# Row sends of a mixture-of-experts router: a wait, inside a phase, for the landing of the first-choice send of the tile ahead

## The chip, the core and the metric

One core of one Trainium2 chip runs one program. The metric is the device time of one execution in microseconds (us). The engines are PE (TensorE), DVE (VectorE), ACT (ScalarE), POOL (GpSimd) and SP (SyncE, which here only issues DMAs). They run side by side and meet only through semaphores. 16 DMA engines move data; SP's DMAs go out on one queue, those of POOL on another, whose descriptors POOL makes itself (the profile calls it software_dynamic).

## The reference, cut to what matters

```python
x = x + 0.5 * L0_moe(layernorm(x))            # 8 experts, 2 choices per token
x = x + L0_attention(layernorm(x))            # keys and values at half length
x = x + 0.5 * L0_moe(layernorm(x))
x = x + 0.5 * L1_ffn(x)     # causal attention, then experts, with residuals inside
x = x + L1_attention(x)                       # causal
x = x + 0.5 * L1_ffn(x)

# the experts of L1_ffn: 16 experts of capacity 2*T/16 = 512 rows
top1, top2 = argmax(logits), argmax(logits without top1)
loc1, loc2 = rank of the token among those of its expert, first and second choices
xin  = rows of xt, token t in row slot(t, choice) of its expert (dropped beyond capacity)
eout = gelu(xin @ fc1 + b1) @ fc2 + b2        # per expert
out  = g1 * eout[slot1] + g2 * eout[slot2]
```

There are 8 x 512 = 4096 tokens of 128 floats, so 32 tiles of 128 tokens.

## The kernel before, in words

The program is a row of blocks: a first routing, experts, attention with half-length keys, experts, causal attention (32 units), experts, two causal attentions as one pipeline (64 units), experts, and the last sums. The change touches the two causal attention blocks alone, at their ends, and both by the same code.

**A unit** is one batch entry (512 tokens) and one of four groups of four heads. `order(u)` writes by hand what each engine does in unit u. PE computes 12 score tiles of unit u (L784, with masks L651) and, unless u is one of the last two, 12 tiles for the row maxima of unit u + 2 (L668). ACT turns each score tile into exponentials (L863), DVE reduces each maxima tile (L1013), and PE multiplies the exponentials with the values (L728). Score and maxima tiles each go through a ring of three PSUM banks, so PE can be at most three tiles ahead of ACT and of DVE. For the next unit, ACT copies the maxima out (nm, L895), POOL splits them into three bf16 parts (`max_split`, L1160 to L1166), and SP writes these into the query rows (L1290); PE waits for that before the first score tile of a unit.

**The routing** of the experts that follow is laid into the same pipeline. Tokens are taken in phases, `SENT_PHASES` = tiles 0 to 7, 8 to 15, 16 to 19, 20 to 23, 24 to 27 and 28 to 31. For each phase DVE chooses experts (`choose`), PE counts ranks (`ranks`), and DVE makes the row numbers (`find_ranks`, slot, L403 and L405). Then `send` lets POOL scatter the rows of each tile from SBUF to `xe_rows` in DRAM, by two indirect DMAs (L418): the one for the first choice raises `first_sent` by 16 when it has landed, the one for the second choice raises `second_sent[j]`. A send is 128 rows of 512 bytes. POOL takes its instructions in order, so what stands behind a send waits for it. Before the first tile of a phase POOL waits for the row numbers and, from the second phase on, for the landing of all second-choice sends of the phase ahead.

**Where the sends stand** is the table `SENT_IN`: tiles 0 to 7 one to a unit, in units -13 to -6 counted from the end; then tiles 8 to 10 in unit -5, 11 to 13 in -4, 14 and 15 in -3, 16 to 19 in -2 and 20 to 23 in -1, behind the unit's other POOL work. Tiles 24 to 27 and 28 to 31 go out behind the last unit, when the row numbers are there. The experts' block begins on SP with `fetch_sent`, which waits for all sends.

Of the kernel before, what the change touches and what calls it, by code (L numbers as in the profile page):

```python
# [408 lines left out]
def send(pool, k, r, j, tiles):  # L409

    s, (a, b) = k.sig, r.phases[j]
    for t in tiles:
        if t == a:
            pool.wait_ge(*s.slots_ready.at(j + 1))
            if j:
                pool.wait_ge(*s.second_sent[j - 1].at(16 * (a - r.phases[j - 1][0])))
        for c, signal in ((0, s.first_sent), (1, s.second_sent[j])):
            pool.indirect_dma_start(k.xe_rows[:, :], bass.IndirectOffsetOnAxis(k.slot[:, c, t:t + 1], 0),  # L418
                                    k.xn[:, t * P:(t + 1) * P], None, bounds_check=r.slots - 1,
                                    oob_is_err=False).then_inc(signal.h, 16)  # L420
# [93 lines left out]
def attention(nc, k, segments, r):  # L514
# [122 lines left out]
    with nc.Block() as block:  # L637
# [486 lines left out]
        def _(pool):  # L1124
# [90 lines left out]
            for u in range(U):  # L1215
# [29 lines left out]
                if r.sent and u - U in SENT_IN:  # L1245
                    phase, first, end = SENT_IN[u - U]
                    send(pool, k, r, phase, range(first, end))
            if r.sent:
                for j in (LAST - 1, LAST):
                    send(pool, k, r, j, range(*r.phases[j]))  # L1250
# [788 lines left out]
```

## Time and profile before

| | us |
|---|---|
| median of 3 runs | 1927.85 (1926.94 to 1928.74) |
| the profiled execution | 1924.9 |
| its span, first to last instruction | 1923.2 |
| PE / DVE / ACT / POOL busy | 1566.6 / 1307.4 / 968.5 / 1075.7 |
| indirect sends on POOL (L418) | 128 instructions, 127.6 us busy |
| mean granted TensorE clock | 0.881 of full |

The span is that of the profiled execution; 1.7 us of its time lie around it. No engine is busy all the time, so a share of busy time says little here; each stage has to be read for itself. A unit's time can be read as the step from one `nm` (L895) to the next. In a wait's row the name behind the arrow is what released the wait; "issue" means that nothing the profile shows was missing, and "remote" that no instruction of this core was found that ended just then.

### The profile page before, as it was taken

The page shows a single profiled execution, that of the slowest core. Times are in us where ns is not written, and L with a number is a line of the kernel's source. Part 1 is how long each engine was busy: PE and PEld are TensorE (multiplying, and loading weights), DVE is VectorE, ACT ScalarE, POOL GpSimd, SP SyncE. Part 2 cuts the span into 40 slices and gives each one's busy share as a digit, 9 for nine tenths or more (in the row PEclk, how much of TensorE's full clock was granted, in tenths as well). Part 3 has the DMA queues.
Part 4 walks back from the last instruction along what each step waited for, and adds up shares of the span by engine and source line. Part 5 has one row for each costly group of instructions (what it writes and reads, how often), then busy time and mean ns, then how long its engine had stood idle before and what let it go on. Part 6 is the DMA issues. An engine that isn't in the chain of part 4 may idle for free. (4 is left out here: it accounts for less than half of the span.)

```text
span 1923.2 us, 46440 instructions
## 1 busy us (share of the span) xinstructions
PE 1566.6 (81%) x17682; PEld 948.8 (49%) x17682; DVE 1307.4 (68%) x3414; ACT 968.5 (50%) x2039; POOL 1075.7 (56%) x1712
## 2 busy tenths in 40 slices
PE   5548888875599998875899599999999998776992
PEld 4532333344345555544576255555555555435772
DVE  7348887883678887856321688888888887765224
ACT  4124667642156676642233177677777766431331
POOL 3446667414477857664355377455666766651552
PEclk9976899987689999985799599999999999865996
DMA  8342323203433322210343433232332323101545
GB/s 295 109 133 86 103 69 94 79 26 94 133 101 113 94 82 83 80 37 19 115 136 102 137 119 91 81 112 82 100 97 82 95 90 97 37 22 55 150 124 159
DMA packets 233187, 188.24 MB, mean 98 GB/s; under 512 B 30035, under 2 KB 221306, under 8 KB 232326
## 3 DMA queue, kind: packets, MB, share of 16 engines
q1 hardware_dynamic: 222582, 166.36, 29.0%
q0 software_dynamic: 10240, 18.89, 3.1%
q8 instruction: 142, 2.33, 0.5%
q14 instruction: 79, 0.65, 0.1%
q10 hardware_dynamic: 144, 0.00, 0.0%
HBM read 104.34 MB, written 80.74 MB: 96 GB/s over the span
## 5 line engine op out<-in xcount | busy, mean ns | idle before, releaser
L1013 DVE TENSOR_REDUCE mx<-PS 128x2 f32<-128x512 f32 (+3 forms) x1408 | 784.6, 612 | 207.1 <-PE PS L651 138.9
L863 ACT ACTIVATE pt<-PS 128x512 f32<-128x512 f32 (+2 forms) x1408 | 668.7, 537 | 323.7 <-PE PS L651 220.2
L668 PE MATMUL PS<-ka,qa 52*128 52x256 bf16 (+3 forms) x2048 | 469.3, 309 | 69.5 <-DVE mx L1013 51.5
L784 PE MATMUL PS<-qa,ka 55*128 55x512 bf16 (+3 forms) x1792 | 465.6, 324 | 31.0 <-DMA qa<-nm 21.2
L728 PE MATMUL PS<-pt,vs 128*32 128x512 f32 (+3 forms) x3584 | 359.4, 487 | 11.7 <-ACT pt L863 7.0
L651 PE MATMUL PS<-mask_q,identh 64*128 64x64 bf16 x3072 | 300.5, 193 | 2.1 <-issue 2.1
L651 PE MATMUL PS<-mask_k,identh 64*128 64x64 bf16 x3072 | 299.5, 192 | 1.6 <-issue 1.6
L784 PEld LDWEIGHTS PS<-qa,ka 55*128 55x128 bf16 x1792 | 167.8, 95 | 261.3 <-ACT pt L863 103.3
L651 PEld LDWEIGHTS PS<-mask_k,identh 64*128 64x128 bf16 x3072 | 249.9, 97 | 53.2 <-issue 10.2
L651 PEld LDWEIGHTS PS<-mask_q,identh 64*128 64x128 bf16 x3072 | 253.4, 98 | 32.5 <-issue 10.6
L668 PEld LDWEIGHTS PS<-ka,qa 52*128 52x128 bf16 x2048 | 172.7, 95 | 101.2 <-DVE mx L1013 65.6
L1160 POOL CAST nm<-nm 16x128 bf16<-16x128 f32 x128 | 35.9, 280 | 324.7 <-ACT nm L895 312.4
L418 POOL DMA_INDIRECT xe_rows<-xn,slot x128 | 127.6, 997 | 84.0 <-DVE slot L405 41.6
L1422 ACT ACTIVATE pt<-PS,f1b 128x512 f32<-128x512 f32 x128 | 87.7, 687 | 154.6 <-PE PS L1386 150.8
L1398 PE MATMUL PS<-pt 128*128 128x128 f32 x1280 | 155.3, 279 | 9.1 <-ACT pt L1422 6.8
L1386 PE MATMUL PS<-pt 128*128 128x512 f32 (+1 forms) x384 | 157.2, 556 | 4.6 <-DVE pt L1479 1.8
L1398 PEld LDWEIGHTS PS<-pt 128*128 128x128 f32 x1280 | 150.7, 196 | 11.7 <-issue 11.1
L1524 POOL DMA_INDIRECT y_rows<-pt,idx x80 | 79.3, 991 | 116.6 <-DVE pt L1489 98.4
L728 PEld LDWEIGHTS PS<-pt,vs 128*32 128x32 f32 x3584 | 83.5, 111 | 92.5 <-issue 40.8
L1386 PEld LDWEIGHTS PS<-pt 128*128 128x128 f32 x384 | 75.0, 206 | 59.7 <-issue 51.5
L1479 DVE TENSOR_SCALAR pt<-PS,l2w,l2b 128x512 f32<-128x512 f32 x32 | 25.9, 810 | 101.1 <-PE PS L1376 98.0
L1516 POOL DMA_INDIRECT pt<-xn_rows,idx x32 | 31.2, 974 | 97.4 <-issue 56.2
(249 smaller groups left out, 2357.0 us busy)
## 6 DMA issues: line engine op xcount, KB each, us to landing
pt<-in_f_w SPq DMA_DIRECT2D x96, 256.0 KB
qa<-q_parts SPq DMA_DIRECT2D x256, 96.0 KB
ka<-k_parts SPq DMA_DIRECT2D x192, 96.0 KB
q_parts<-parts SPq DMA_DIRECT2D x32, 384.0 KB
k_parts<-parts SPq DMA_DIRECT2D x24, 384.0 KB, 2.6
xn<-y_rows SPq DMA_DIRECT2D x32, 256.0 KB, 3.1
hid<-y_rows SPq DMA_DIRECT2D x32, 256.0 KB, 3.6
q_parts<-parts SPq DMA_DIRECT2D x32, 256.0 KB
```

The lines of the kernel that those rows point to most:

```text
L418: pool.indirect_dma_start(k.xe_rows[:, :], bass.IndirectOffsetOnAxis(k.slot[:, c, t:t + 1], 0), k.xn[:, t * P:(t + 1) * P], None, bounds_c ...
L651: mm = pe.matmul(PS[:, bank, col + j * HALF:col + (j + 1) * HALF], k.identh[half * HALF:(half + 1) * HALF, j, :], table[half * HALF:(half ...
L668: mm = pe.matmul(PS[:, bank, i * n:(i + 1) * n], k.qa[rows, b % 2, g, h // 2, qb * P:(qb + 1) * P], k.ka[rows, b % 2, g, h // 2, 0:n], sta ...
L728: mm = pe.matmul(PS[32 * h:32 * h + 32, O_BANK, q0:S], k.vs[:, g, kb, h, :], k.pt[:, u % 2, at[c] + i * n:at[c] + (i + 1) * n], start=(kb ...
L784: mm = pe.matmul(PS[:, bank, i * n:(i + 1) * n], k.ka[rows, b % 2, g, h // 2, kb * P:(kb + 1) * P], k.qa[rows, b % 2, g, h // 2, q0:S], st ...
L863: nc.scalar.activation(k.pt[:, u % 2, at[c]:at[c] + len(heads) * n], PS[:, SC_BANK + c % RING, 0:len(heads) * n], ACT.Exp, scale=SCORE_SCA ...
L1013: nc.vector.tensor_reduce(out, PS[:, MX_BANK + t % RING, 0:len(heads) * n] .rearrange("p (h n) -> p h n", n=n), AX.X, ALU.max).then_inc(s. ...
L1160: pool.tensor_copy(hi, full).then_inc(s.nm_hi.h, 1)
L1386: pe.matmul(PS[:, H_BANK + f, 0:capacity], k.w1[:, par, f * P:(f + 1) * P], k.xeT[:, par, 0:capacity], start=True, stop=True).then_inc(s.h ...
L1398: mm = pe.matmul(PS[:, Y_BANK + par, t * P:(t + 1) * P], k.hT[:, par, f, t * P:(t + 1) * P], k.w2[:, par, f, :], start=(f == 0 and t == 0) ...
L1422: nc.scalar.activation(k.hT[:, e % 2, f, 0:capacity], PS[:, H_BANK + f, 0:capacity], GELU, bias=w.b1[:, e * FC + f:e * FC + f + 1]).then_i ...
L1524: pool.indirect_dma_start(k.y_rows[:, :], bass.IndirectOffsetOnAxis(k.idx[:, 1, n:n + 1], 0), k.ys[e % RING_E][:, t, :], None).then_inc(s. ...
```

## The change

Inside a phase, each tile but the phase's first one gets a wait on POOL ahead of its two sends, in all phases but the last (tiles 28 to 31). `first_sent` must have reached 16 times the tile's number, that is, all first-choice sends of the tiles ahead must have landed.

```diff
             pool.wait_ge(*s.slots_ready.at(j + 1))
             if j:
                 pool.wait_ge(*s.second_sent[j - 1].at(16 * (a - r.phases[j - 1][0])))
+        elif j < len(r.phases) - 1:
+            pool.wait_ge(*s.first_sent.at(16 * t))
         for c, signal in ((0, s.first_sent), (1, s.second_sent[j])):
             pool.indirect_dma_start(k.xe_rows[:, :], bass.IndirectOffsetOnAxis(k.slot[:, c, t:t + 1], 0),
                                     k.xn[:, t * P:(t + 1) * P], None, bounds_check=r.slots - 1,
```

Each of the two blocks gets 23 such waits: 7 for phase 0, 7 for phase 1, and 3 for each of phases 2, 3 and 4. No instruction that computes or moves data is added, removed or put elsewhere.

## Rows read from the trace of the kernel before

**Rows 1.** The page, costliest groups: the sends (busy, mean ns, idle before, releaser).

```profile
L418 POOL DMA_INDIRECT xe_rows<-xn,slot x128 | 127.6, 997 | 84.0 <-DVE slot L405 41.6
```

**Rows 2.** Windows: stretch, length, busy us of PE, PEld, DVE, ACT, POOL, clock, DMA.

```profile
745.00:815.00 70.00, 60.27 (x906) 35.11 (x907) 54.55 (x129) 42.68 (x95) 45.89 (x82) 0.93 0.29 89
815.00:885.00 70.00, 53.01 (x578) 29.38 (x579) 38.99 (x145) 29.72 (x66) 40.23 (x52) 0.76 0.10 33
...
1555.00:1640.00 85.00, 75.11 (x1131) 43.56 (x1131) 66.00 (x151) 53.64 (x119) 58.00 (x101) 0.94 0.29 88
1645.00:1722.00 77.00, 59.34 (x639) 31.84 (x632) 46.89 (x168) 33.22 (x73) 43.85 (x59) 0.78 0.09 28
```

**Rows 3.** Waits, 815 to 885 us: who, for whom, us in total, times, longest.

```profile
ACT pt L863 <- remote: 18.4, 6, 7.3
...
DVE mx L1013 <- remote: 9.8, 3, 4.4
...
ACT xfT L215 <- remote: 6.9, 1, 6.9
...
DVE rw L390 <- remote: 5.6, 1, 5.6
...
ACT nm L895 <- remote: 3.1, 1, 3.1
```

**Rows 4.** Waits, 1645 to 1722 us, the same columns.

```profile
ACT pt L863 <- remote: 22.0, 6, 5.9
...
DVE mx L1013 <- remote: 10.3, 3, 6.2
...
ACT xfT L215 <- remote: 5.8, 1, 5.8
```

**Rows 5.** Waits, 745 to 815 us: the only row with "remote".

```profile
DVE mx L1013 <- remote: 0.5, 1, 0.5
```

**Rows 6.** Waits, 1555 to 1640 us: the only such row of ACT.

```profile
ACT pt L863 <- remote: 1.6, 1, 1.6
```

**Rows 7.** Timeline of POOL: first-choice sends of tiles 4 and 5 (start, us, idle before).

```profile
779.52 1.00 POOL L418 DMA_INDIRECT xe_rows<-xn,slot  x1 [0.78 <-POOL parts L1140]
...
783.89 1.01 POOL L418 DMA_INDIRECT xe_rows<-xn,slot  x1 [0.16 <-issue]
```

**Rows 8.** Timeline of POOL: first-choice sends of tiles 8 and 9, the next max_split.

```profile
817.20 1.00 POOL L418 DMA_INDIRECT xe_rows<-xn,slot  x1 [1.62 <-issue]
...
819.78 0.97 POOL L418 DMA_INDIRECT xe_rows<-xn,slot  x1 [0.30 <-issue]
...
828.80 0.28 POOL L1160 CAST nm<-nm 16x128 bf16<-16x128 f32 x1 [4.21 <-ACT nm L895]
```

**Rows 9.** Timeline of ACT in the same burst.

```profile
823.08 0.38 ACT L863 ACTIVATE pt<-PS 128x256 f32<-128x256 f32 x1 [3.67 <-remote]
```

**Rows 10.** The DMA view, 839 to 843 us: bytes moved, in 40 slices of 0.1 us.

```profile
GB/s 0 0 0 0 271 292 41 0 0 0 0 0 0 0 0 0 0 410 246 0 0 0 0 0 0 0 0 0 0 0 466 98 0 0 0 0 0 0 0 0
```

**Rows 11.** Timeline of POOL: last send of tile 13, the max_splits behind and next.

```profile
840.45 0.97 POOL L418 DMA_INDIRECT xe_rows<-xn,slot  x1 [0.30 <-issue]
841.41 0.28 POOL L1160 CAST nm<-nm 16x128 bf16<-16x128 f32 x1
...
855.32 0.28 POOL L1160 CAST nm<-nm 16x128 bf16<-16x128 f32 x1 [7.17 <-ACT nm L895]
```

**Rows 12.** Timeline of POOL: last send of tile 23, first of tile 24.

```profile
1718.90 0.97 POOL L418 DMA_INDIRECT xe_rows<-xn,slot  x1 [0.30 <-issue]
1721.85 1.06 POOL L418 DMA_INDIRECT xe_rows<-xn,slot  x1 [1.98 <-DMA xe_rows<-xn,slot]
```

**Rows 13.** Timeline of POOL: first send of the last phase.

```profile
910.53 1.14 POOL L418 DMA_INDIRECT xe_rows<-xn,slot  x1 [15.56 <-DVE slot L405]
```

**Rows 14.** The score matmuls (L784), 815 to 885 us: all that ended PE's idle time.

```profile
  ACT pt L863: 11.8, 9
  issue: 4.6, 11
```

## The prediction

> **What bounds the kernel now.** I read the page first. No engine is busy all through, so the question is only what happens where the 128 sends stand [rows 1]. The sends lie in two places, one at the end of each causal attention. So the second view is the table of windows over these ends. Each end has a stretch with isolated sends (one tile, two sends, per unit) and one with bursts (two to four tiles in a row). From the one to the other ACT's busy time falls from 42.7 to 29.7 us of 70 in the first block, and from 53.6 of 85 to 33.2 of 77 in the second; DVE and PE fall too, and the DMA engines are busy for 10% [rows 2]. So in the bursts no compute engine is the bound, and neither is DMA bandwidth. Part of that is sound: the last two units have no maxima tiles, and the routing of the last phases stands there. The third view, the waits, shows the rest. With the bursts ACT waits 18.4 + 6.9 + 3.1 = 28.4 us in the first block for something that the profile can't name [rows 3], and 22.0 + 5.8 = 27.8 us in the second [rows 4]. With isolated sends, 8 tiles in each block, the whole is 0 us for ACT in the first [rows 5], where only DVE has such a row, and 1.6 us in the second [rows 6]. DVE shows the same: 15.4 and 10.3 us in the bursts, 0.5 us outside in the first block [rows 3 to 5].
>
> The fourth view, the timelines, shows how one such stall looks. In the burst of tiles 8 to 10 ACT sits idle for 3.67 us and runs at 823.08 [rows 9]. By the pitch of the tiles (819.78 - 817.20 = 2.58 us [rows 8], two sends each, so 1.29 us from send to send) the last two sends of this burst start at about 822.4 and 823.6. So while POOL sends one tile after another, work that is ready on other engines isn't taken up, for several microseconds, and it goes on near the time at which some send lands. I can't tell from the trace what carries the stall. What I can read is its price: the bursts of tiles 8 to 23 cost ACT 28.4 / 16 = 1.8 and 27.8 / 16 = 1.7 us per tile, isolated tiles at most 1.6 / 8 = 0.2.
>
> The Trainium skill speaks against this. "SBUF — State Buffer", section "SBUF: two separate sides", says that engine ports and DMA ports are apart, so that a transfer can't slow a compute instruction; the exception it names is the port pair that VectorE and GpSimd share. The trace shows ACT stalled as well as DVE, which that exception doesn't cover. By the page the stalls would have another cause than the transfers in flight, and spacing the sends would give nothing: that is the rival "no change" below.
>
> **The change part by part.** It adds 23 waits per block and removes nothing.
>
> *Waits that are met anyway.* Tiles 1 to 7 are sent one to a unit; the closest two start 783.89 - 779.52 = 4.37 us apart [rows 7]. Tiles 11 and 14 open a unit. These 9 waits per block find their landing done and cost nothing, as long as a landing takes under 4.37 us.
>
> *Waits inside a burst.* These are tiles 9, 10, 12, 13, 15, 17, 18, 19, 21, 22 and 23, so 11 per block, and 3 more (25 to 27) behind the last unit. Now the pitch is the 2.58 us of rows 8. When does a send land? Its bytes move 1.55 us after its start: the send of 840.45 fills the slices at 842.0 and 842.1, and the two before it show the same spacing [rows 10, 11]. And there is one place where POOL already waits for nothing but a landing: tile 24's first send starts 1721.85 - 1718.90 = 2.95 us after the start of the send on whose landing it waited [rows 12]. That is the price of a wait of this kind, waking and issuing included. So the pitch of a tile goes from 2.58 to 2.95 us, by 0.37 us, if the wait for the first-choice send wakes POOL at once. The other end: the second-choice send of the tile ahead starts some 1.3 us after the first and is still in flight then. If POOL, like ACT in the stalls, is only released when that one has landed as well, the pitch is 1.3 + 2.95 = 4.25 us, by 1.7 us more than now. The cost of the wait is so between 0.37 and 1.7 us; it can't be below nothing, since it only holds POOL back. I take 0.37, because the released engines of rows 9 ran on in mid-burst, with further sends in flight.
>
> *What is queued behind.* POOL's next work behind a burst is max_split. Behind tiles 8 to 10 it waits 4.21 us for ACT anyway [rows 8], which covers 2 x 0.37 (and, just, 2 x 1.7). Behind tiles 14 and 15 it waits 7.17 us [rows 11]. Behind tiles 11 to 13 it starts with no idle time, at 841.41, so it comes 0.7 to 3.4 us later; who waits for it is SP and then PE's first score tile of the unit after, and that is far: the next max_split is at 855.32, and PE's scores never waited for these rows in the whole stretch [rows 11, 14]. Without that cover it would cost 0.7 us per block. Behind tiles 16 to 23 POOL has only more sends. Tiles 24 to 27 would end 3 x 0.37 later plus what tiles 21 to 23 pass on, 2.2 us in all, at most 10; the last phase waits 15.56 us for DVE's row numbers anyway [rows 13]. The last phase itself has no new wait, so what the experts' block waits for isn't held back. So on POOL, SP and the last phase the change costs nothing.
>
> *What the spacing gives.* The only thing to win is the stall. Between two prices per tile (1.75 us at a pitch of 2.58, at most 0.2 us, say 0.1, at 4.37 and more) I go on a straight line: at 2.95 us a tile costs 1.75 - 1.65 x 0.37 / 1.79 = 1.41 us, so each wait gives 0.34 us, and 22 of them 7.5 us. There is a reason for more than the line: the rings of three tiles let ACT and DVE catch up after a short stop and not after a long one, and the bytes of two tiles now come 1.29 us apart throughout a burst, and 1.29 + 0.37 = 1.66 us apart at every wait with the change. I add a third and take 10 us. At the other end, pitch 4.25, the line gives 22 x 1.54 = 34 us.
>
> The sum against the profiled execution: 1924.9 - 10 + 0 = 1914.9 us. The median of the runs shown lies 2.95 us above that execution, so against the median it is 1927.85 - 10 = 1917.8 us.
>
> **The rivals.**
>
> *A, the forecast:* the pitch grows little, the stalls shrink a little. 4 to 16 us off, 1917.8.
>
> *B, isolated tiles:* POOL is released late, as ACT is, and the sends go out as in rows 7. 34 us off: 1894. For it speaks that ACT's and DVE's stalls of 3 to 7 us [rows 3, 4] must come from signals that are held up, and POOL's wait is such a signal too. Against it, that a landing is itself what seems to end a stall.
>
> *C, no change:* the landing is early. Bytes move 1.55 us after the start and the next tile starts at 2.58, so if POOL takes the wait up ahead of time, it never sees it, and the pitch stays; or the pitch grows and the same number of sends stalls the others for as long in total, since each is as long in flight as before. Then 1927.85. The skill's "DMA: Bandwidth & Descriptors", section "Anatomy of one DMA — SWDGE (gpsimd) path", gives about 2.0 us fixed plus bytes / 436e3 us per DMA; for 64 KB that would be an estimated 2.15 us, also under 2.58. Rows 12 have 2.95 for landing, waking and issuing.
>
> *D, slower:* the stalled share stays and the bursts grow. The bursts of tiles 8 to 23 last some 40 us per block (16 tiles at 2.58, less the idle time between), and ACT stalls for 28.4 of them, 0.7. If that share holds for the added time as well, 22 x 0.37 x 0.7 = 5.7 us are lost: 1933.5. At a pitch of 4.25 it would be 22 x 1.7 x 0.7 = 26 us, 1954. It decides from the point where ACT's unnamed waits in the two burst stretches go over the present 28.4 + 27.8 us: then the stall belongs to POOL's making of sends for its length, and not to their closeness.
>
> **How the numbers follow.** A measurement of this kernel can tell about 0.2%, 3.9 us, from no change. Chances: A 0.37, B 0.2, C 0.26, D 0.17. The bottom of A lies at the limit, so I give faster 0.55, same 0.28, slower 0.17. The point is A's, 1917.8. The range leaves out D but for its lower edge and takes in all of B, with 4 us for the line: 1890 to 1933.5. The likeliest case alone is 1912 to 1924.
>
> **What would show it right or wrong.** In the timeline of POOL, the pitch of tiles 8 to 10: 2.95 (A), 4.25 (B), 2.58 (C). In the waits of the two burst stretches, ACT's "remote" sum: about 46 to 50 us in both blocks for A, under 15 for B, 56 for C, over 60 for D. The units with bursts should be shorter, and the idle time before 910.53's send should still be over 5 us. It would be wrong if POOL's wait were held up in one burst and not in another, or if the freed time in the last units were given back in the wait for the last phase's row numbers, which DVE makes behind everything else.

## The result and the profile after

| | us |
|---|---|
| before, median of 5 runs | 1928.74 (1926.94 to 1937.12) |
| after, median of 5 runs | 1911.12 (1908.49 to 1915.54) |
| ratio, 95% interval | 0.9898, 0.9873 to 0.9922 |
| the profiled execution after, its span | 1912.18, 1910.5 |
| PE / DVE / ACT / POOL busy after | 1556.0 / 1307.4 / 968.9 / 1077.0 |
| mean granted TensorE clock after | 0.887 of full |

The change makes the kernel 1.0% faster, 17.6 us between the medians and 12.7 us between the two profiled spans. In the first block the bursts stand at nearly the same times as before; in the second they start 2 us and end 8 us earlier. The same windows hold them in both kernels. Of the page of the kernel after, the row of the sends, to be read against [rows 1] (busy, mean ns, idle before, main releaser):

```profile
L420 POOL DMA_INDIRECT xe_rows<-xn,slot x128 | 129.0, 1008 | 78.6 <-issue 42.3
```

The idle time before the sends did not grow, it is 78.6 us after 84.0: the waits inside the bursts were paid by a shorter wait ahead of the last phases. The windows of the kernel after, the same stretches as [rows 2] (stretch, length, busy us of PE, PEld, DVE, ACT, POOL, clock, DMA share, GB/s):

```profile
815.00:885.00 70.00, 55.38 (x629) 30.63 (x620) 43.98 (x157) 32.96 (x71) 40.64 (x54) 0.79 0.10 33
...
1645.00:1722.00 77.00, 54.36 (x654) 32.33 (x654) 54.98 (x200) 33.30 (x73) 46.20 (x60) 0.84 0.10 30
```

In the first block ACT gets through 33.0 us of work in the 70 us where it got through 29.7, DVE 44.0 for 39.0. In the second DVE does 55.0 for 46.9, in part because routing of the last phases already falls into the window. The waits of the kernel after, 815 to 885 us (who, for whom, us in total, times, longest), to be read against [rows 3]:

```profile
ACT pt L865 <- remote: 7.5, 6, 2.3
DVE mx L1015 <- remote: 6.6, 3, 4.6
DVE rw L390 <- remote: 6.2, 1, 6.2
ACT xfT L215 <- remote: 5.9, 2, 3.1
...
ACT osb L903 <- remote: 3.4, 1, 3.4
...
ACT logits L224 <- remote: 1.2, 1, 1.2
```

And those of 1645 to 1722 us, against [rows 4]:

```profile
ACT pt L865 <- remote: 7.1, 5, 2.3
...
ACT osb L903 <- remote: 4.2, 1, 4.2
...
ACT xfT L215 <- remote: 2.7, 1, 2.7
```

ACT's waits for something unnamed went from 28.4 to 18.0 us in the first block and from 27.8 to 14.0 us in the second, 24.2 us less in both. The longest single wait for a score tile fell from 7.3 to 2.3 us in the first block. DVE's such waits are 12.8 us (15.4 before) in the first block and 2.5 us (10.3 before) in the second. POOL's timeline shows the burst of tiles 8 to 10 after, to be read against [rows 8] (start, us, idle before):

```profile
818.17 1.01 POOL L420 DMA_INDIRECT xe_rows<-xn,slot  x1 [0.16 <-issue]
...
821.20 0.97 POOL L420 DMA_INDIRECT xe_rows<-xn,slot  x1 [0.75 <-issue]
...
824.24 0.96 POOL L420 DMA_INDIRECT xe_rows<-xn,slot  x1 [0.80 <-issue]
...
831.27 0.28 POOL L1162 CAST nm<-nm 16x128 bf16<-16x128 f32 x1 [4.80 <-ACT nm L897]
```

The three tiles start 3.03 and 3.04 us apart. max_split behind them still waits for ACT, 4.80 us.

Where the time was won, unit by unit: the last six units, each from ACT's first exponential of a unit to that of the next (the last one to the start of its own last exponential), in us, worked out from ACT's timeline. Unit -6 stands ahead of the bursts, and its length scatters without any change: 15.2 and 11.5 us in the second profile of the kernel before, further down.

| units from the end | -6 | -5 | -4 | -3 | -2 | -1 | sum |
|---|---|---|---|---|---|---|---|
| first block, before | 13.7 | 16.9 | 9.2 | 17.5 | 17.4 | 14.0 | 88.8 |
| first block, after | 15.2 | 16.4 | 9.5 | 13.3 | 18.2 | 10.9 | 83.5 |
| second block, before | 11.8 | 17.4 | 8.8 | 17.3 | 19.0 | 14.1 | 88.4 |
| second block, after | 14.5 | 15.0 | 8.3 | 13.4 | 14.7 | 11.1 | 76.9 |

Together 5.3 + 11.5 = 16.8 us. From the end of the first block to the start of the second, and behind the second, 1.1 and 2.9 us are given back; with some tenths in the units ahead, this leads to the 12.7 us of the two spans.

### The profile page after: what moved, and what is told of

It is laid out like the page before. It is cut to its first block and busy times, and to the rows that moved or that the text cites. A ratio compares the mean times of both kernels' runs of the same rounds, so it can differ in the third digit from the quotient of the medians.

```text
span 1910.5 us, 46442 instructions
## 1 busy us (share of the span) xinstructions
PE 1556.0 (81%) x17682; PEld 947.9 (50%) x17682; DVE 1307.4 (68%) x3414; ACT 968.9 (51%) x2039; POOL 1077.0 (56%) x1712
## 5 line engine op out<-in xcount | busy, mean ns | idle before, releaser
L786 PE MATMUL PS<-qa,ka 55*128 55x512 bf16 (+3 forms) x1792 | 462.2, 322 | 33.6 <-DMA qa<-nm 26.5
L730 PE MATMUL PS<-pt,vs 128*32 128x512 f32 (+3 forms) x3584 | 353.1, 484 | 3.7 <-issue 3.0
L420 POOL DMA_INDIRECT xe_rows<-xn,slot x128 | 129.0, 1008 | 78.6 <-issue 42.3
L1400 PEld LDWEIGHTS PS<-pt 128*128 128x128 f32 x1280 | 152.4, 197 | 13.4 <-issue 12.2
```

The source lines that it names most:

```text
L730: mm = pe.matmul(PS[32 * h:32 * h + 32, O_BANK, q0:S], k.vs[:, g, kb, h, :], k.pt[:, u % 2, at[c] + i * n:at[c] + (i + 1) * n], start=(kb ...
L786: mm = pe.matmul(PS[:, bank, i * n:(i + 1) * n], k.ka[rows, b % 2, g, h // 2, kb * P:(kb + 1) * P], k.qa[rows, b % 2, g, h // 2, q0:S], st ...
L1400: mm = pe.matmul(PS[:, Y_BANK + par, t * P:(t + 1) * P], k.hT[:, par, f, t * P:(t + 1) * P], k.w2[:, par, f, :], start=(f == 0 and t == 0) ...
```

## The experiments

Twelve runs on four chips. The kernel before was measured beside each of them, and it fell into two groups that I had not reckoned with: about 1928 us on two of the chips (as for the prediction), about 1867 us on the two others. I call them chips with and without stalls, because on the second kind no profile has a single unnamed wait in the bursts. Each of the four chips was met in one sitting, so whether the stalls belong to the chip or to its condition at the time isn't shown. Which chip gave the result above I don't know; I call it the first chip. A ratio is always to the kernel before on the same chip.

### Chips without stalls: four kernels side by side

**Spacing without a wait for landing.** If the gain comes from the spacing of the sends, two small POOL instructions in place of each of the new waits should bring it too. They are put where the change has its wait. The wait in the lines is for POOL's own step ahead, not for a landing, and the sends behind it show 0.17 us of idle time, put down to nothing:

```diff
-        elif j < len(r.phases) - 1:
-            pool.wait_ge(*s.first_sent.at(16 * t))
+        elif j < len(r.phases) - 1:
+            pool.wait_ge(*steps.step.at(steps.n))
+            pool.tensor_scalar(k.pdev[:, :, 0:12], <24 columns of ident>, 1.0, 0.0, ALU.mult, ALU.add)
+            pool.tensor_scalar(k.ptmp[:, :, 0:12], <24 columns of ident>, 1.0, 0.0,
+                               ALU.mult, ALU.add).then_inc(steps.step.h, 1)
+            steps.n += 1
```

> The kernel before, without the new waits; instead POOL does two small operations of its own (24 columns, about 0.28 us each) ahead of the same tiles, so that the pitch of the tiles in a burst grows to about the 3.0 us that the changed kernel has, and POOL never stops its run-ahead for a landing. Theory closeness (the stall of the other engines comes from sends being packed, and any spacing thins it): 10 to 18 us faster than before, like the changed kernel, and ACT's unnamed waits in the two burst stretches sum to about 32 us in place of 56. Theory wait (it is the stop for the landing itself that lets the others go on): no gain, 1928, ACT's unnamed waits stay near 56 us. Theory burst length (rival D): 5 us slower.

Measured: 1874.01 us against 1866.35, ratio 1.0045 (1.003 to 1.006). A small loss, and nothing to win: with no stall in the kernel before, this run tells nothing about stalls.

**Wait for both landings.** The change, and a wait for the second-choice send of the tile ahead as well:

```diff
         elif j < len(r.phases) - 1:
             pool.wait_ge(*s.first_sent.at(16 * t))
+            pool.wait_ge(*s.second_sent[j].at(16 * (t - a)))
```

> The changed kernel, and each waiting tile also waits for the landing of the second-choice send of the tile ahead; pitch 1.3 + 2.95 = 4.25 us. Theory closeness: the stall per tile falls further, by the straight line of the prediction to nearly nothing, ACT's unnamed waits in the burst stretches under 15 us in all; another 10 to 15 us faster than the changed kernel (1897 to 1901), unless the longer bursts now hold back max_split or the last phase. Theory that the total time in flight counts: the same as the changed kernel, 1911. Theory burst length: slower than the changed kernel by 10 us or more.

Measured: 1911.68 us, ratio 1.0242 (1.0221 to 1.0263). POOL's timeline of this kernel (start, us, idle before) shows the pitch:

```profile
821.16 1.08 POOL L421 DMA_INDIRECT xe_rows<-xn,slot  x1 [0.17 <-issue]
...
825.61 0.98 POOL L421 DMA_INDIRECT xe_rows<-xn,slot  x1 [2.09 <-DMA xe_rows<-xn,slot]
...
829.95 0.97 POOL L421 DMA_INDIRECT xe_rows<-xn,slot  x1 [2.08 <-DMA xe_rows<-xn,slot]
```

4.45 and 4.34 us from tile to tile, near the 4.25 us that the prediction worked out as its upper end (5.0 and 5.2 us in another burst of the same edit). Here the trace names the landing as what POOL waited for. Both covers of the prediction are used up at this pitch: in the first block PE waits twice, for 8.6 us in all, for the query rows that come out of max_split, and tile 28, the first of the last phase, goes out 4.58 us behind tile 27 with no wait for DVE's row numbers left.

**The wait in all phases, the last too.**

```diff
-        elif j < len(r.phases) - 1:
+        else:
             pool.wait_ge(*s.first_sent.at(16 * t))
```

> The changed kernel with the wait in the last phase too (tiles 29 to 31). The experts' block waits for these sends, so 3 x 0.45 = 1.35 us are added on the path at each of two places, 2.7 us in all, and little is won, since DVE and PE have little to do beside them but the marks. Expected 1 to 3 us slower than the changed kernel; if the stalls of DVE's marks count, up to 2 us faster.

Measured: 1883.6 us, ratio 1.0079 (1.0057 to 1.01), a loss of 17 us where the same waits gained on the chips with stalls. Its six last units take 68.9 and 68.5 us; those of the kernel with dropped rows (below, and as fast as before) take 63.1 and 63.2. So the waits of the bursts cost some 5.6 us per block here. Most of it one line shows: PE's waits for the query rows, 795 to 860 us (who, for whom, us in total, times, longest), with the waits in all phases:

```profile
PE PS L786 <- DMA qa<-nm: 4.5, 1, 4.5
```

The same of the kernel with dropped rows:

```profile
PE PS L784 <- DMA qa<-nm: 1.0, 1, 1.0
```

PE waits 3.5 us longer for the query rows that come out of max_split, of the 5.9 us that the first block loses (3.7 of 5.3 us in the second), and max_split comes late. What the rest goes to was not traced. POOL's timeline of the kernel with the waits, from the last send of tile 10 to max_split behind tiles 11 to 13:

```profile
814.57 0.97 POOL L420 DMA_INDIRECT xe_rows<-xn,slot  x1 [0.30 <-issue]
815.51 0.28 POOL L1162 CAST nm<-nm 16x128 bf16<-16x128 f32 x1
...
820.78 1.08 POOL L420 DMA_INDIRECT xe_rows<-xn,slot  x1 [0.17 <-issue]
...
825.62 0.98 POOL L420 DMA_INDIRECT xe_rows<-xn,slot  x1 [2.47 <-DMA xe_rows<-xn,slot]
...
830.86 0.28 POOL L1162 CAST nm<-nm 16x128 bf16<-16x128 f32 x1
```

Behind tiles 8 to 10, where the kernel after had 4.80 us of idle time on its chip, max_split starts with none, and so it does behind tiles 11 to 13. It starts with none behind tiles 8 to 10 in the kernel with dropped rows too, which has no waits: this cover is missing on the chip, not eaten up by the change. And a wait can cost more than 0.45 us: tile 12 starts 4.84 us behind tile 11, because this one landing was late. From one max_split to the other it is 830.86 - 815.51 = 15.35 us; with dropped rows and no waits it is 12.70. So the cover of the prediction (POOL waits for ACT anyway) is there only as long as the stalls hold ACT back.

**Rows dropped.** To tell the data from the making of the sends, phases 1 to 4 get a bound that drops their rows; this kernel leaves out nearly all rows of tiles 8 to 27 and so doesn't compute what the reference asks for:

```diff
-                                    k.xn[:, t * P:(t + 1) * P], None, bounds_check=r.slots - 1,
+                                    k.xn[:, t * P:(t + 1) * P], None, bounds_check=0 if 0 < j < 5 else r.slots - 1,
```

> The kernel before, with the rows of the sends of phases 1 to 4 (tiles 8 to 27) left out: the bound on the row number is 0 there, so POOL goes through the same sends at the same pitch, and hardly a byte moves; the experts compute on other rows. Theory that the data on its way stalls the others: the stalls go, ACT's unnamed waits under 10 us in the burst stretches, and 25 us or more faster than before. Theory that POOL's making of a send, or its signalling, does it: the stalls stay, 50 to 60 us of unnamed waits of ACT and 1928.

Measured: 1866.79 us, ratio 1.0008 (0.9997 to 1.002). No difference: on a chip without stalls the rows' bytes cost nothing. It also gives the length of the units without stalls: 63.1 and 63.2 us per six, for 88.8 and 88.4 before on the first chip. That is 25.5 us per block, 51 of the 61 us that lie between the two kinds of chip.

### A chip with stalls: the changed kernel and the one before again

Both kernels, unchanged, on another chip, since the first four runs had put in doubt whether the stalls are there at all.

> The changed kernel once more, unaltered. In the four runs just seen the kernel before took 1866 us and no engine had an unnamed wait; where the prediction was measured it took 1928 us with 56 us of unnamed waits of ACT. Theory that the chip (or its condition) brings the stall and the change only thins it: where before takes about 1866 us and has no unnamed waits, the changed kernel is 8 to 16 us slower; where before takes about 1928 us, it is 15 to 20 us faster. Theory that the gain is the kernel's own: faster by 1% in both.

Measured: 1901.05 us against 1927.76, ratio 0.9867 (0.9829 to 0.9904).

> The kernel before, unaltered, for a profile beside that of the changed kernel. Theory chip: either 1866 us with no unnamed wait in the bursts, or 1928 us with 50 us or more of them for ACT; nothing between. Theory of chance from run to run: anything between.

Measured: one time of 1919.91 us, not against anything. Its waits show the stalls again: ACT 27.6 us unnamed in the first block, 22.9 in the second. The waits from 815 to 885 us, first of the kernel before again:

```profile
ACT pt L863 <- remote: 22.8, 8, 6.6
ACT xfT L215 <- remote: 4.8, 1, 4.8
...
DVE rw L390 <- remote: 4.1, 1, 4.1
```

Then of the changed kernel on that chip:

```profile
DVE rw L390 <- remote: 4.8, 1, 4.8
ACT osb L903 <- remote: 2.6, 1, 2.6
ACT logits L224 <- remote: 1.6, 2, 1.1
...
ACT pt L865 <- remote: 1.1, 2, 0.9
```

ACT's sum falls from 27.6 to 5.3 us there, and the twelve last units of the two blocks take 149.8 us for 177.3. So the reading of the prediction holds: what the waits take away is unnamed waiting in the bursts.

The pitch isn't 3.03 us everywhere. POOL's timeline of the changed kernel on this chip, the first-choice send of tile 15:

```profile
850.21 0.97 POOL L420 DMA_INDIRECT xe_rows<-xn,slot  x1 [2.36 <-DMA xe_rows<-xn,slot]
```

It starts 4.65 us behind that of tile 14, because a landing was late. Of the 22 waits inside bursts three show 1.8 us or more of idle time on this chip, one in the profile of the result, two in the third run below.

### A second chip with stalls: what it is that helps

Four kernels beside 22 runs of the kernel before, median 1927.52 us.

**Spacing again**, the same kernel as above, now where there is something to win:

> The same kernel as spaced (two small POOL operations in place of each wait). Two chips have been seen: on one the kernel before takes 1866 us without unnamed waits, on the other 1928 us with them. If this job meets the second: theory closeness says 1905 to 1912 us, like the waits at the same pitch; theory wait says 1928, no gain. If it meets the first: 1874 us again, 0.45% slower.

Measured: 1911.18 us, ratio 0.9935 (0.991 to 0.9959). POOL's timeline (start, us, idle before):

```profile
812.70 1.01 POOL L424 DMA_INDIRECT xe_rows<-xn,slot  x1 [0.16 <-issue]
...
815.57 1.01 POOL L424 DMA_INDIRECT xe_rows<-xn,slot  x1 [0.17 <-issue]
...
818.43 0.99 POOL L424 DMA_INDIRECT xe_rows<-xn,slot  x1 [0.17 <-issue]
```

A pitch of 2.87 us with no wait for any landing, 0.29 more than before, and ACT's unnamed waits (7.0 of them for score tiles, 4.9 for xfT) are 11.9 us:

```profile
DVE mx L1019 <- remote: 7.4, 4, 4.8
ACT pt L869 <- remote: 7.0, 6, 2.3
ACT xfT L215 <- remote: 4.9, 2, 3.0
```

Spacing alone is enough for a gain of 0.65%. The landing isn't needed for it. The twelve last units take 160.9 us.

**Rows dropped again.**

> The same kernel as dropped_rows (sends of tiles 8 to 27 carry almost no rows). On the chip with the stalls: theory data says they go and the time falls by 25 us or more, below 1903; theory signals and making of sends says 1928 within 5 us and unnamed waits of ACT near 50 us. On the chip without stalls: 1866 us, as before.

Measured: 1929.54 us, ratio 1.0019 (1.0001 to 1.0036). The DMA view of 819 to 826 us, the sends' queue (packets, MB, share), shows that the bytes are gone:

```profile
q0 software_dynamic: 128, 0.00, 1.3%
```

In the kernel before, the burst of tiles 8 to 10 (817 to 826 us) moves 0.37 MB there. The six units last 88.5 and 92.0 us, as long as before, and the waits from 815 to 885 us still hold

```profile
ACT xfT L215 <- remote: 7.7, 1, 7.7
ACT pt L863 <- remote: 7.6, 4, 5.1
DVE mx L1013 <- remote: 7.1, 2, 6.3
```

So it isn't the rows' bytes, nor their writes to DRAM, that hold up the others. It is something that a send has with and without rows: the making of its descriptors, the packets without bytes (128 in this stretch), or the signals at its end. ACT's own sum is smaller here (15.3 and 14.3 us in the two blocks) while the units are as long, so this sum is a rough measure of the stall; the units' length is the safer one.

**Waits in the later phases only.** Phases 0 and 1 go out as before, the waits stand in phases 2 to 4 (the two last units and behind them):

```diff
-        elif j < len(r.phases) - 1:
+        elif 1 < j < len(r.phases) - 1:
             pool.wait_ge(*s.first_sent.at(16 * t))
```

> The changed kernel with the waits only in phases 2, 3 and 4 (tiles 16 to 27), where no max_split stands behind the sends. On the chip with the stalls it keeps the gain of units -2 and -1 and loses that of units -5 to -3: about 12 us faster than before. On the chip without stalls the loss of the waits should be gone, if it comes from max_split being late in units -5 to -3: within 3 us of before.

Measured: 1913.68 us, ratio 0.9932 (0.9915 to 0.9949), 0.6 of the whole gain (0.9892, below) at the point estimates. The units, in us, first block (to be read against the table above and the next run):

| units from the end | -6 | -5 | -4 | -3 | -2 | -1 |
|---|---|---|---|---|---|---|
| waits in phases 2 to 4 only | 13.4 | 17.9 | 8.9 | 17.2 | 16.8 | 8.5 |
| waits everywhere, the same chip | 13.4 | 14.7 | 8.3 | 12.6 | 16.1 | 8.8 |

A burst without waits keeps its stall, and a burst with waits loses some of its own: the effect is local. The second block shows the same, 17.5 us in unit -3 and 8.5 in unit -1 with the waits in phases 2 to 4 only. Unit -1, with the longest burst of the kernel before (four tiles behind four), falls from about 14 to 8.5 us; unit -2, with as many tiles, loses hardly anything, and I can't say why.

**The changed kernel a third time.**

> The changed kernel. On the chip with the stalls 1901 to 1911 us against 1928. On the chip without stalls, where only the form with waits in all phases has been run (0.8% slower): 0.6 to 0.75% slower than before, 1877 to 1880 us, since PE waits for the maxima's rows in units -4 and -3.

Measured: 1903.66 us, ratio 0.9892 (0.9865 to 0.9919). ACT's unnamed sum is 7.4 and 6.4 us. Three measurements with stalls give 0.9898, 0.9867 and 0.9892.

### Chips without stalls once more

**Spacing by three instructions**, for a pitch like that of the waits; the added line:

```diff
             pool.tensor_scalar(k.pdev[:, :, 0:12], <24 columns of ident>, 1.0, 0.0, ALU.mult, ALU.add)
+            pool.tensor_scalar(k.gap[:, :], k.ident[:, 0:4], 1.0, 0.0, ALU.mult, ALU.add)
```

> As spaced, with a third small POOL operation (4 columns) ahead of each tile, so that the pitch in a burst comes to 3.0 to 3.1 us, that of the waits, where spaced had 2.87 and gave 0.65% on a chip with stalls against 1.08% of the waits. Theory closeness: on a chip with stalls 0.9 to 1.2% faster than before, the same as the waits. Theory that the stop for the landing adds something of its own: 0.65% as spaced. On the chip without stalls: 0.6 to 0.8% slower.

Measured: 1878.26 us against 1867.35, ratio 1.0061 (1.0041 to 1.0082). POOL's timeline:

```profile
802.61 1.01 POOL L425 DMA_INDIRECT xe_rows<-xn,slot  x1 [0.16 <-issue]
...
805.64 1.02 POOL L425 DMA_INDIRECT xe_rows<-xn,slot  x1 [0.17 <-issue]
...
808.69 1.01 POOL L425 DMA_INDIRECT xe_rows<-xn,slot  x1 [0.17 <-issue]
```

The pitch is 3.03 and 3.05 us, that of the changed kernel. But the chip was one without stalls, so the question, whether a wait for landing gives more than spacing at the same pitch, stays open.

**Both landings again.**

> The changed kernel with the wait for both sends of the tile ahead, pitch 4.3 to 4.4 us. On the chip without stalls it was 2.4% slower (1911.7). On a chip with stalls: theory closeness by the straight line says the stalls are nearly gone and 3% would be won by that, less the 2.4% that the late max_split and last phase cost where no stall hides them: 1905 to 1920. Theory that stalls cost only what exceeds those losses: about 1912, the time of the chip without stalls, since with no two tiles close together the two chips should hardly differ in the bursts and differ by some 35 us elsewhere: 1912 to 1945.

Measured: 1910.86 us, ratio 1.0233 (1.0212 to 1.0255), the same loss as on the other chip without stalls.

### The pitch and the time, side by side

| pitch in a burst, us | chips with stalls | chips without |
|---|---|---|
| 2.58, before | 1 | 1 |
| 2.87, spaced | 0.9935 | 1.0045 |
| 3.03 as a rule, first landing (or spaced by three) | 0.9867 to 0.9898 | 1.0079 (all phases), 1.0061 (spaced by three) |
| 4.3 to 5.2, both landings | not run | 1.0233, 1.0242 |

Without stalls a wider pitch costs, little at 2.87 and 2.3 to 2.4% at 4.3 and over; with stalls it gives more than it costs, 0.65% for 0.29 us and 1.0 to 1.3% for 0.45 us.

Two measures of the stall, both blocks together, in the profiled executions with stalls, us:

| | twelve last units | ACT's unnamed waits | span |
|---|---|---|---|
| before; before again | 177.2; 177.3 | 56.2; 50.5 | 1923.2; 1918.2 |
| rows dropped, pitch of before | 180.5 | 29.6 | 1933.3 |
| waits in phases 2 to 4 only | 163.0 | 32.9 | 1913.4 |
| spaced | 160.9 | 27.1 | 1907.4 |
| the change: result; again; third | 160.3; 149.8; 150.8 | 32.0; 11.0; 13.8 | 1910.5; 1899.5; 1900.7 |

The span goes roughly with the units. It doesn't go with ACT's sum: that falls to 29.6 us with the rows dropped, and nothing is won.

## Why the prediction was right

**What bounds the kernel: right.** The unnamed waits beside the bursts are the price of closely packed sends: spacing alone shrinks them, and bursts left as they were keep them (waits in the later phases only). The other kind of chip shows it from the far side: the same six units, 88.8 us here, last 63.1 us where nothing stalls (read from the kernel with dropped rows, which is as fast there as the kernel before).

**The objection by the skill's page.** By the Trainium skill, "SBUF — State Buffer", section "SBUF: two separate sides", transfers don't slow compute instructions. With the rows dropped the stall stayed, so the page's rule isn't contradicted by this stall. What the prediction drew from it, that then spacing would give nothing, is contradicted: spacing gave 0.65% with no change to the data moved.

**Price of a wait: right, a little low.** 2.95 us of pitch were expected, from the last phase's one wait [rows 12]; the burst shows 3.03, so a wait costs 0.45 and not 0.37 us. The landing itself can be read on chips without stalls, where the profile has it: median 2.3 us after the start of a send, the least 2.1. As a median that is before the 2.58 us of the old pitch; the pitch grows all the same, so rival C (the wait is never seen) fails: 21 of the 22 waits show as 0.60 to 0.84 us of idle time where there were 0.30. The other one took 1.81 us. The prediction had named a wait held up in one burst and not in another as a sign of being wrong, and this does occur, one to three times in 22; no term of the sum had it.

**Cover on POOL: right for this chip, and thinner than stated.** Behind tiles 8 to 10 the cover is 4.80 us [rows 8 had 4.21]. Ahead of the last phase it shrank as foreseen in the first block, from 15.56 us [rows 13] to

```profile
907.29 1.13 POOL L420 DMA_INDIRECT xe_rows<-xn,slot  x1 [10.52 <-DVE slot L405]
```

In the second block it is 6.87 us, and on the second chip with stalls the first block has 3.02 us left, under the 5 us that the prediction wanted to see. The cover held, with less room than thought.

The step that failed is the one for max_split behind tiles 11 to 13: "PE's scores never waited for these rows in the whole stretch" [rows 14]. In the changed kernel they do, 815 to 885 us:

```profile
PE PS L786 <- DMA qa<-nm: 1.1, 1, 1.1
```

With the stalls shorter, ACT and PE are ready sooner, and PE has to wait for POOL's max_split. It is 1.1 us in each of the two blocks, so 2.2 us that the sum had at nothing, and 1.2 to 1.7 us per block on the two other chips. On a chip without stalls, with the waits in all phases, this wait grows by 3.5 and 3.7 us and is the larger part of what the two blocks' last units lose.

**What the spacing gives: the mechanism right, the size too small.** The sum's term of 10 us was mis-sized: the medians lie 17.6 us apart. A straight line from 1.75 us of stall per tile at a pitch of 2.58 to 0.1 at 4.37 gave 0.34 us per wait, 7.5 us, rounded up to 10. ACT's unnamed waits fell by 24.2 us in the measured execution, and by 22.3 + 17.2 = 39.5 us on the second chip. Against 22 waits that is 1.1 us and more per wait.

By the units, the kernel before is 51 us above the one without stalls in the two blocks, and the change takes away 17 of them on this chip and some 27 on the two others, a third to a half, where the line gives a quarter for 0.45 of 1.8 us. So the curve is steeper than a line at its start; the landings that came late may be part of it. The 24 us don't all reach the end: 16.8 us show in the units of the two profiled executions, and 12.7 us at the end (17.6 by the medians).

By the sign it had set itself (46 to 50 us of ACT's sum for A, under 15 for B) the result, 32.0 us, lies between A and B, with A's pitch; the two other chips give 11.0 and 13.8 us, B's sum at A's pitch. The sign was a poor one, since the kernel with dropped rows has 29.6 us and gains nothing. Rival B's mechanism, POOL released late and tiles as far apart as in rows 7, isn't what happened, save for the few waits that were held up.

That the time lies in the range says little: the range is 43.5 us wide and holds no change and a small loss as well. The direction, the pitch and the place of the gain carry the prediction; the point, 1917.8, is 6.7 us off.

A second term had no place in the sum: the granted clock. The windows of the kernel before (columns as in rows 2), with a stall in 836 to 843:

```profile
836.00:843.00 7.00, 2.43 (x41) 1.36 (x37) 2.30 (x4) 2.05 (x6) 5.55 (x9) 0.86 0.14 45
843.00:850.00 7.00, 6.59 (x64) 4.32 (x64) 4.94 (x17) 2.30 (x7) 3.95 (x5) 0.65 0.11 36
```

The same windows of the kernel after:

```profile
836.00:843.00 7.00, 6.48 (x95) 3.87 (x89) 6.57 (x18) 4.96 (x11) 4.73 (x6) 1.00 0.12 37
843.00:850.00 7.00, 5.47 (x93) 3.19 (x94) 6.73 (x27) 2.18 (x6) 5.14 (x9) 1.00 0.13 40
```

Before, PE gets only 2.43 us of work in the 7 us of the stall, and in the next 7 us the granted clock is 0.65 of full, so part of them at 1.2 and not at 2.4 GHz. After, PE stays busy, and the clock stays at full. So here a stall is paid twice, while it lasts and by the slower PE behind it. Other windows go the other way (822 to 829 has 0.74 before and 0.64 after). On the whole the clock is a little higher: 0.76 to 0.79 in 815 to 885, 0.78 to 0.84 in 1645 to 1722, and 0.878 to 0.886 in seven executions of the kernel before against 0.889 to 0.892 in four of the changed one, on the second chip. PE is busy for 10.6 us less (1566.6 to 1556.0) with the same 17,682 matmuls, but the kernel before had 1556.7 us in its other profile, so this difference can't be put down to the change. What the clock gives of the 17.6 us wasn't measured by itself.

**The other rivals.** D (slower, because POOL's sends stall the others for their length) falls on chips with stalls: its sign, over 60 us in ACT's sum, was 32.0. But the kernel can get slower by another way, the one through max_split, on the chips without stalls. The prediction had that term at 0.7 us per block; there PE's wait grows by 3.5 and 3.7 us.

**What stays open.** What carries the stall is not found. It isn't the bytes. On the chips with stalls the profile holds fewer records of semaphore updates (27,373 to 27,777, some 31,590 on the others). Nearly all that are missing are updates by DMAs: 17,753 of them in the kernel before, 21,714 in the one with dropped rows on a chip without stalls. So the profile there has landing times for 0 or 16 of the 128 sends, for 24 to 96 on the others. Something about these signals differs, in the chip or only in what is recorded; whether it causes the stalls or only goes with them isn't shown. The changed kernel itself wasn't run on a chip without stalls, only with the wait in all phases. A kernel that is best on both kinds wasn't found; the one with waits in the later phases alone keeps some 0.6 of the gain and spares the bursts ahead of the max_splits, but it wasn't run on the other kind.

## What to carry to other kernels

Where ready work on other engines stands still beside a burst of indirect sends from POOL, put the sends a few tenths of a microsecond further apart, by a wait or by POOL work that is needed anyway, and do so where nothing urgent is queued behind them on POOL. When a cover is credited to an engine that waits for another anyway, ask whether that other is itself late because of what the change repairs. And measure on more than one chip: here the sign of the spacing's effect depends on it.

## What the hardware showed that I had not expected

- The same kernel takes 1928 us on some chips and 1867 on others, 3.2%, each repeatable to some tenths of a per cent. 51 of the 61 us lie in twelve units of the 96, beside the bursts. Nearly all of the other 10 arise ahead of the first causal block, whose first exponential comes at 541.8 us in the kernel before and at 531.0 in the one with dropped rows. There, too, the kernel before has unnamed waits beside other indirect sends of POOL (`y_rows`): 26.5 us of DVE and 9.3 us of ACT in 70 to 120 and 450 to 500 us, where a chip without stalls has none. The change doesn't touch these.
- A burst of indirect sends at a pitch of 2.58 us per tile holds up ACT, DVE and with them PE on the one kind of chip, for up to 7.3 us at a time (7.7 when the sends carry no bytes). At 2.87 us the twelve last units take 160.9 us for 177.2 and 177.3.
- Two POOL instructions on 128 x 24 between two tiles add 0.29 us to the pitch, a third of 128 x 4 another 0.17; a wait for the first-choice landing adds 0.45, or up to 2.3 where that landing is late (4.84 us of pitch). On the chips without stalls, where the profile has them, the sends land 2.2 to 2.4 us after their start in the median and 4.7 us at most.
